# Three-layer graph convolution on one core: the third layer gathers rows stored as high and low f32r parts

## The reference

```python
def _gcn_layer(h_in, W, b, src, dst, norm_edge, n_nodes):
    h = h_in @ W
    msg = h[src] * norm_edge[:, None]
    agg = jax.ops.segment_sum(msg, dst, num_segments=n_nodes)
    return agg + b
...
deg = jax.ops.segment_sum(jnp.ones_like(dst, dtype=x.dtype), dst, num_segments=n)
dinv = jnp.where(deg > 0, jax.lax.rsqrt(deg), 0.0)
norm_edge = dinv[src] * dinv[dst]
h = x
for W, b in ((W1, b1), (W2, b2), (W3, b3)):
    h = jax.nn.relu(_gcn_layer(h, W, b, src, dst, norm_edge, n))
...
x = _layernorm(x + h, axis=-1)
```

## Time and profile before

| | us |
|---|---|
| median of three runs | 2473.04 |
| span of the profiled execution | 2904.7 |
| first layer's windows and before | up to 1165 |
| second layer | 1165 to 2346 |
| third layer | 2346 to 2904.7 |

### The profile page before, as it was taken

How to read it: one execution, slowest core, us unless ns; L and a number is a source line. 1 busy time by engine, 2 the same in 40 slices (tenths; PEclk the granted TensorE clock), 3 DMA queues, 4 the chain that set the end, 5 groups by cost and what they waited for, 6 DMA issues and landing times.

```text
span 2904.7 us, 33204 instructions
## 1 busy us (share of the span) xinstructions
PE 2414.3 (83%) x10765; PEld 1582.4 (54%) x10765; DVE 846.7 (29%) x1155; ACT 721.3 (25%) x1501; POOL 1757.6 (61%) x1768
## 2 busy tenths in 40 slices
PE   7866687788888789789788888979888789899897
PEld 6744465556565566344343444434444367777676
DVE  8875122112121211222222222222221223333333
ACT  6411222222122221122121222212221023333332
POOL 4366655556555564666667666666666756555553
PEclk9778899999899999899899898989999889999999
DMA  5445555555555555667666676767767645556663
GB/s 184 140 127 185 162 146 159 150 153 160 150 152 155 160 156 153 189 205 207 203 200 208 190 211 203 215 193 204 210 202 224 199 137 157 150 147 184 183 195 97
DMA packets 219959, 508.70 MB, mean 175 GB/s; under 512 B 38444, under 2 KB 106915, under 8 KB 219827
## 3 DMA queue, kind: packets, MB, share of 16 engines
q0 software_dynamic: 117216, 365.08, 44.1%
q1 hardware_dynamic: 83955, 109.08, 11.1%
q10 hardware_dynamic: 18656, 32.75, 3.7%
HBM read 433.60 MB, written 73.16 MB: 174 GB/s over the span
## 4 chain that ended last, share of the span: by engine, by line
PE 52%; another core or an unknown queue 22%; issue 10%; DVE 6%; ACT 4%; POOL 3%; DMA 1%; ACTq 1%; POOLq 1%; DVEq 0%; SPq 0%
PE ps_acc L1668 11%; PE ps_d L1668 9%; PE ps_o L1717 6%; PE ps_acc L1664 5%; PE ps_d L1767 4%; PE ps_h L1756 4%; PE ps_T L1756 3%; POOL rows L739 3%; PE ps_e L1738 3%; PE ps_l L1738 3%; ACT rows_r L1447 2%; PE ps_d L1620 2%; PE ps_h L1708 2%; DVE sel L956 1%
## 5 line engine op out<-in xcount | busy, mean ns | idle before, releaser
L739 POOL DMA_INDIRECT rows<-table,idx x1249 | 1240.8, 993 | 709.2 <-issue 382.6
L739 POOL DMA_INDIRECT rows<-table_parts,idx x483 | 476.5, 987 | 336.1 <-PE ps_acc L1664 152.7
L1668 PE MATMUL ps_acc<-rows,sel 128*128 128x512 f32 (+2 forms) x1496 | 615.9, 532 | 61.8 <-DVE acc L1042 27.7
L956 DVE SCALAR_TENSOR_TENSOR sel<-ps_e,firsts,dstT 128x1152 f32<-128x1152 f32 (+1 forms) x214 | 302.5, 1414 | 1223.6 <-remote 430.6
L1668 PE MATMUL ps_d<-rows,sel 128*128 128x512 f32 (+2 forms) x1190 | 541.4, 571 | 13.0 <-DMA rows<-table,idx 9.2
L1668 PEld LDWEIGHTS ps_acc<-rows,sel 128*128 128x128 f32 x1496 | 300.8, 208 | 226.5 <-issue 172.4
L1668 PEld LDWEIGHTS ps_d<-rows,sel 128*128 128x128 f32 x1190 | 235.8, 206 | 171.1 <-issue 134.0
L1664 PE MATMUL ps_acc<-rows,sel 128*128 128x256 bf16 (+1 forms) x1533 | 252.3, 281 | 81.9 <-DVE acc L1042 66.8
L1717 PE MATMUL ps_o<-low,hT 128*128 128x512 f32 (+1 forms) x784 | 295.9, 523 | 27.2 <-ACT hT L1365 14.4
L1767 PE MATMUL ps_d<-big 128*128 128x256 bf16 x1470 | 241.1, 280 | 28.8 <-issue 28.6
L1756 PE MATMUL ps_T<-pairs_r,rows_r 128*128 128x512 f32 x686 | 236.2, 460 | 33.2 <-ACT rows_r L1447 21.6
(11 more groups left out here) (192 smaller groups left out, 1663.3 us busy)
## 6 DMA issues: line engine op xcount, KB each, us to landing
rows<-table,idx POOLq DMA_INDIRECT x1249
table<-made SPq DMA_DIRECT2D x49, 256.0 KB
acc<-table SPq DMA_DIRECT2D x49, 256.0 KB
built<-big SPq DMA_DIRECT2D x30, 384.0 KB
low<-built ACTq DMA_DIRECT2D x30, 384.0 KB
built_bytes<-big SPq DMA_DIRECT2D x54, 192.0 KB
low<-built_bytes ACTq DMA_DIRECT2D x54, 192.0 KB
table_parts<-big SPq DMA_DIRECT2D x24, 384.0 KB
```

The lines of the kernel that those rows point to most:

```text
L739: pool.indirect_dma_start(out=to, out_offset=None, in_=its[0:nodes, :], in_offset=bass.IndirectOffsetOnAxis(ap=idx[:, of, k:k + 1], axis=0 ...
L956: v.scalar_tensor_tensor(to[:, k:k + FRONT, :], numbers.unsqueeze(1).broadcast_to([P, FRONT, P]), firsts[:, bass.ds(t, 1)], dstT[:, bass.d ...
L1668: return mm(to[:, 0:w], sel[:, k, :], rows_of[phase][:, k, 0:w] if first is None else first, start=start, stop=stop)
```

## The change

The second layer's product leaves PSUM in two steps: ScalarE writes `ps_o * dinv`, rounded to f32r, as the high part, and VectorE writes what is left (`keep_low`) as the low part, for one tile, two windows later. SP stores both as one row of 512 words in `table_pairs`. The third layer gathers rows of 2 KB from there instead of 1 KB, its selection is made in f32r, and a slot is one f32r matmul of 512 columns into a PSUM bank whose halves VectorE adds up (`take_pairs`). The own row is no longer loaded in the third layer; a matmul of `pairs_r` with the identity adds it after the second slot. The six wide steps and the copy for `late` go. As the rows now fill `rows`, the ring moves into `low`, and the room for loaded blocks shrinks from two blocks to one: each piece has its own buffer and is loaded one block ahead.

```diff
+        rows_pairs = rows_r[:, :].rearrange("p (k w) -> p k w", w=2 * C)
+        with nc.sbuf_tensor("sel_r", [P, SLOTS, P], F32R) as sel_r:
...
-        with nc.sbuf_tensor("pairs_r", [P, 2, T, C], F32R) as pairs_r:
+        with nc.sbuf_tensor("pairs_r", [P, T, 2, C], F32R) as pairs_r:
...
-        whole = xs
-        low_r, high_r = pairs_r[:, 0, :, :], pairs_r[:, 1, :, :]
+        pairs = pairs_r[:, :, :, :].bitcast(F32).rearrange("p t i c -> p t (i c)")
...
                     def store(t, s):
-                        sp.wait_ge(made_ready, s + 1)
-                        its = made[:, 0:WIDTH[phase + 1]]
                         if phase == 1 and per == 1:
-                            its = whole[:, bass.ds(t, 1), :].rearrange("p a c -> p (a c)")
-                        sp.dma_start(table[phase + 1][bass.ds(t * P, P), :], its).then_inc(stored, 16)
+                            sp.wait_ge(pairs_ready, t + 1)
+                            sp.dma_start(table_pairs[bass.ds(t * P, P), :],
+                                         pairs[:, bass.ds(t, 1), :].rearrange("p a w -> p (a w)")).then_inc(stored, 16)
+                        else:
+                            sp.wait_ge(made_ready, s + 1)
+                            sp.dma_start(table[phase + 1][bass.ds(t * P, P), :], made[:, 0:WIDTH[phase + 1]]).then_inc(stored, 16)
...
-            def gather(phase, k, of, nodes=T * P, in_parts=False):
+            def gather(phase, k, of, nodes=T * P, in_parts=False, in_pairs=False):
                 to, its = rows_of[phase][:, k, 0:WIDTH[phase]], table[phase]
                 if in_parts:
                     to, its = rows_parts[:, k, :], table_parts[phase]
+                if in_pairs:
+                    to, its = rows_pairs.bitcast(F32)[:, k, :], table_pairs
                 g = next(i for i, s in enumerate(GROUPS) if k in s)
                 pool.indirect_dma_start(
                     out=to, out_offset=None, in_=its[0:nodes, :],
                     in_offset=bass.IndirectOffsetOnAxis(ap=idx[:, of, k:k + 1], axis=0)).then_inc(landed[g], 16)
...
+            def take_pairs(t, n, ps):
+
+                v_.wait_ge(window_done, n + 1)
+                v.scalar_tensor_tensor(y1[:, :], ps[:, 0:C], dinv[:, t:t + 1], b3b[:, :], ALU.mult, ALU.add).then_inc(y_g_scaled, 1)
+                v_.wait_ge(y_g_scaled, t + 1)
+                v.scalar_tensor_tensor(y1[:, :], ps[:, C:2 * C], dinv[:, t:t + 1], y1[:, :], ALU.mult, ALU.add).then_inc(sum_taken, 1)
...
-            def take_apart(turn, t, n):
-
-                its = whole[:, bass.ds(t, n), :]
-                v.tensor_copy(high_r[:, bass.ds(t, n), :], its).then_inc(highs_ready, 1)
-                v_.wait_ge(highs_ready, turn + 1)
-                v.tensor_tensor(low_r[:, bass.ds(t, n), :], its, high_r[:, bass.ds(t, n), :], ALU.subtract).then_inc(pairs_ready, 1)
+            def keep_low(t):
+
+                v_.wait_ge(highs_ready, t + 1)
+                v.scalar_tensor_tensor(pairs_r[:, t, 1, :], ps_o[:, 0:C], dinv[:, t:t + 1], pairs_r[:, t, 0, :],
+                                       ALU.mult, ALU.subtract).then_inc(pairs_ready, 1)
...
-                    take_sum(phase, n - 1, n - 1, True, ps_sums[1 - odd] if phase > 0 else ps_acc)
+                    if phase == 2:
+                        take_pairs(t - 1, n - 1, ps_sums[1 - odd])
+                    else:
+                        take_sum(phase, n - 1, n - 1, True, ps_sums[1 - odd] if phase > 0 else ps_acc)
                     if not last:
                         indices(next_base, 1 - odd)
                     elif phase < 2:
                         v.tensor_copy(idx[:, 1 - odd, :], early_src[:, :]).then_inc(idx_ready, 1)
-                    prepare(n, t, base, 1, sel_parts if in_parts else sel)
+                    prepare(n, t, base, 1, to)
+                    if phase == 1 and t >= 2:
+                        keep_low(t - 2)
...
                 def to_next(phase):
                     n = nth_of_windows(phase + 1, 0)
                     base = base_of(1)
-                    prepare_early(n, 0)
+                    to = sel_r if phase == 1 else sel
+                    prepare_early(n, 0, to)
                     take_sum(phase, n - 1, n - 1, True, ps_sums[(n - 1) % 2] if phase > 0 else ps_acc)
                     indices(base, 1 - WINDOWS[phase + 1] % 2)
-                    prepare_early(n, 1)
+                    prepare_early(n, 1, to)
+                    if phase == 1:
+                        for t in range(T - 2, T):
+                            keep_low(t)
...
-                        if o == 2 and not first:
-                            n = PAIRS_OF[0][1]
-                            v_.wait_ge(stored, 16 * T + 16 * n * i)
-                            take_apart(i - 1, n * (i - 1), n)
...
                 def finish_gathered(g, b):
                     t = GROUP * g + b
                     n = nth_of_windows(2, t)
-                    finish(t, n + 2, n + 2, of_gather(g, b))
+                    normalize_rest(sum_taken, n + 2, res[:, :], res_in, t, of_gather(g, b), y3[:, :], y3_free, y_ready)
...
                 act.wait_ge(o_done, s + 1)
                 if phase == 1 and per == 1:
-                    to = whole[:, bass.ds(t, 1), :].rearrange("p a c -> p (a c)")
-                else:
-                    to = made[:, 0:w]
-                    act.wait_ge(made_free, s + 1)
+                    for of in range(2):
+                        if t == OVER_BYTES[of]:
+                            act.wait_ge(tile_stored[of], 16 * len(PIECES) * (DENSE // 2 + 1))
+                    act.sem_inc(act_step, 1)
+                    nc.scalar.activation(pairs_r[:, t, 0, :], ps_o[:, 0:w], ACT.Copy, scale=dinv[:, t:t + 1]).then_inc(highs_ready, 1)
+                    return
+                act.wait_ge(made_free, s + 1)
                 act.sem_inc(act_step, 1)
-                nc.scalar.activation(to, ps_o[:, 0:w], ACT.Copy, scale=dinv[:, bass.ds(t, 1)]).then_inc(made_ready, 1)
+                nc.scalar.activation(made[:, 0:w], ps_o[:, 0:w], ACT.Copy, scale=dinv[:, bass.ds(t, 1)]).then_inc(made_ready, 1)
...
-            def piece_in(j, into, piece):
+            def piece_in(j, piece):
 
                 lo_h, hi_h = PIECES[piece]
-                its = blocks[into][:, lo_h:hi_h, :].rearrange("p h d -> p (h d)")
-                return its.bitcast(U8)[:, 0:(hi_h - lo_h) * P] if in_bytes(j) else its
-
-            def load_blocks(j, into, piece):
+                n = (hi_h - lo_h) * P
+                return loaded[piece].bitcast(U8)[:, 0:n] if in_bytes(j) else loaded[piece][:, 0:n]
+
+            def load_blocks(j, piece):
                 lo_h, hi_h = PIECES[piece]
                 its = built_bytes if in_bytes(j) else built
-                act.dma_start(piece_in(j, into, piece), its[j * P:(j + 1) * P, lo_h * P:hi_h * P]).then_inc(blocks_in[into], 16)
-
-            def widen(g, x, more=True):
+                act.dma_start(piece_in(j, piece), its[j * P:(j + 1) * P, lo_h * P:hi_h * P]).then_inc(blocks_in[piece], 16)
+
+            def widen(g, x):
 
                 d, piece = divmod(x, len(PIECES))
                 lo_h, hi_h = PIECES[piece]
-                whole_x = DENSE_OF * len(PIECES) * g + x
-                act.wait_ge(blocks_in[d % 2], 16 * len(PIECES) * (DENSE_OF // 2 * g + d // 2 + 1))
-                if not (isinstance(g, int) and whole_x < 2):
+                j = DENSE_OF * g + d
+                whole_x = len(PIECES) * j + piece
+                act.wait_ge(blocks_in[piece], 16 * (j + 1))
+                if whole_x >= 2:
                     act.wait_ge(dense_piece, whole_x - 1)
                 act.sem_inc(act_step, 1)
                 nc.scalar.activation(ring[piece % 2][:, 0:hi_h - lo_h, :].rearrange("p h d -> p (h d)"),
-                                     piece_in(DENSE_OF * g + d, d % 2, piece), ACT.Copy).then_inc(widened, 1)
-                if more:
+                                     piece_in(j, piece), ACT.Copy).then_inc(widened, 1)
+                if j + 1 < DENSE:
                     act.wait_ge(widened, whole_x + 1)
-                    load_blocks(DENSE_OF * g + d + 2, d % 2, piece)
+                    load_blocks(j + 1, piece)
...
-                act.wait_ge(made_free, T + 1)
-                nc.scalar.activation(made[:, 0:C], ps_o[:, 0:C], ACT.Copy, scale=dinv[:, T - 1:T]).then_inc(late_ready, 1)
                 for of in range(2):
                     act.wait_ge(tile_stored[of], 16 * len(PIECES) * (DENSE // 2 + 1))
-                for piece in range(len(PIECES)):
-                    load_blocks(1, 1, piece)
                 widen(0, 0)
...
+                if in_pairs:
+                    return mm(to[:, 0:2 * C], sel_r[:, k, :], rows_pairs[:, k, :] if first is None else first, start=start, stop=stop)
...
+                    if own is not None and k == ORDER[1]:
```

(13 more changed lines are left out.)

118 lines of the change are left out of this document (65 added, 53 removed).

## The result

| | before | after |
|---|---|---|
| median | 2474.24 us (4 runs) | 2408.46 us (4 runs, 2405.69 to 2411.2) |
| ratio, 95% interval | | 0.9726 (0.9712 to 0.9739) |
| profiled span | 2904.7, profiled again 2471.5 | 2405.7 |

The change saves 65.8 us, 2.7%. The forecast was 2426 us, 47 us less, with a range of 2388 to 2466: the range holds the result, the gain is 19 us larger than forecast.

The account below looks back on a forecast made before the run. The prediction took TensorE to bound the third layer. Its terms, -70 slots, +4 GpSimd, +8 doubled rows, +7 ScalarE, +7 seam, -3 second layer, sum to -47 us: 2473 to 2426 us, range 2388 to 2466.

Parts of the forecast that it names:

- Slots, -70: Third layer, TensorE: 357 slots fall from 0.44 to 0.23 us, less 5 us for own-row matmuls; net -70 us.
- Rival E: Third-layer slots: an f32r matmul takes two passes, 0.46 us, after all; 2497 us, chance 0.05.
- GpSimd, +4: Third layer: gathers at 19.6 us a window are no longer covered by TensorE's 19.2; +4 us, between 0 and 8.
- Doubled rows, +8: Third-layer DMA queues: doubled row bytes make windows with bf16 blocks exceed TensorE's time; +8 us, between 0 and about 48.
- Rival C: Third layer: DMA engines become the bound and their packets do not overlap; 2450 us, chance 0.22.
- ScalarE's stops, +7: Third layer, between windows: TensorE waits longer for block widening behind a square root; +7 us, between 0 and 14.
- The seam, +7: Between layers two and three: tile 47's store waits for its low half, delaying the first gather; +7 us, -1.5 to 10.
- The second layer, -3: Second layer: without VectorE's wide splits, gathers beside them are no longer slowed; -3 us, between -15 and +3.
- mostly slack: Second layer: the delay of some 3 us at each of five wide-split places was taken as mostly slack.
- B: Full gain: gathers quicker than 1.25 us unprofiled, no DMA bound, seam partly hidden, splits' room wholly used; 2395 us, chance 0.12.
- A: The forecast itself, whole kernel: 2426 us, own range 2405 to 2448, chance 0.52.
- D: Third layer: block loads issued only one block ahead land late behind full gather queues; 2502 us, chance 0.09.

Follow-up runs that it names:

- experiment 2: Changed kernel with the third layer's slots as f32 matmuls of 256 columns over the high halves alone, except each window's first slot: 2464.35 us, ratio 0.9951.
- Experiment 3: Changed kernel with one gather less in each third-layer window but the first: 2399.57 us, ratio 0.9682.
- Experiment 4: Changed kernel gathering 1 KB rows instead of 2 KB in the third layer, as many gathers and still 512-column matmuls: 2407.5 us, ratio 0.9714.
- experiment 8: Changed kernel with ScalarE widening two pieces of each third-layer group before the square roots instead of behind them: 2405.52 us, ratio 0.9715.
- Experiment 5: Changed kernel with tile 47's low half made before the third layer's first selection instead of behind window 48's sum: 2400.66 us, ratio 0.9698.
- experiment 7: Changed kernel with five wide copy and tensor_tensor pairs put back on VectorE in the second layer: 2418.71 us, ratio 0.9776.
- experiment 6: Changed kernel without the own-row matmul in the third layer: 2405.79 us, ratio 0.9719.
- experiment 12: Changed kernel with tile 47's low part early and ScalarE widening first, plus dense-tile one-hots by eight short comparisons instead of two: 2373.56 us, ratio 0.9591.

## Why the prediction was right or wrong

**Slots, -70: right.** A slot is one record at 0.23 us; TensorE's busy time in the layer fell by 66 us between the two comparable profiles; experiment 2 gives 71 us back to TensorE. Rival E is out by the rows.

**GpSimd, +4: right mechanism, its window read too short.** "It is late next" held, and more than that: it never pauses again. The term had 329 gathers; there are 337, since eight of them started ahead of the stretch that was counted, so a window is 16.0 x 1.25 = 20.1 us and not 19.6. And the first rows were not there early: the slack counted for the first windows had gone at the seam. Experiment 3 prices GpSimd with the seam at some 9 us, where the forecast had 4 + 7.

**Doubled rows, +8: wrong.** Experiment 4 measures it at 1 us, within the error. The step that failed took five microseconds at 303 GB/s for a limit. (The 6.9 us a window of its first estimate are 6.7 by its own factors, 1.92 MB at 3.5 us; nothing hangs on it.) Late in the layer the page shows 344 and 347 GB/s in two slices of 60 us, and TensorE waits 1.3 us for rows in both together. Landing takes a gather 4.7 us (median) from its issue against 3.8 for all of the kernel before's, and that is hidden, as groups are asked for ahead. The Trainium skill (DMA: Bandwidth & Descriptors, Where 436 GB/s comes from) has about 358 GB/s as the limit of a core; the slices just named stay below it, and by that rule the term would have been nothing. Rival C is out.

**ScalarE's stops, +7: right as a term, worth less.** They grew by 6.7 us, as the forecast had it, but experiment 8 takes 7.6 us of them away, gets 7.3 us more of waits for rows, and leaves the layer's length as it was: a stop is covered by GpSimd, which fetches on through it.

**The seam, +7: right.** Experiment 5 gives 7.8 us back with the mechanism of the forecast, the store of tile 47 behind window 48's selection. It is right partly by luck: the clean profile shows that the old pause was 2.87 us and not the 13.3 of the earlier trace rows, and that the rows now start only 1.3 us ahead of the dense matmuls. A second part was not foreseen: TensorE waits for rows there and its granted clock is 0.62 over the first 13 us of the layer, where it was 0.87. By stretches it is 0.50 to 0.52, the lower level (1.2 GHz), from 1967 to 1977 us, after TensorE had been busy for 6.5 of the 12 us up to 1967; before the change the clock was back at 1.00, the upper level (2.4 GHz), 6 us into the layer. An estimate of the price is (0.87 - 0.62) x 13, some 3 us. With the rows 8.6 us sooner (experiment 5) the same 13 us show 0.87 again.

```profile
1979.00:1992.00 13.00, 12.95 (x51) 10.67 (x51) 1.54 (x2) 4.46 (x3) 9.70 (x11) 0.87 0.63 187
```

```profile
1964.00:1977.00 13.00, 9.13 (x21) 6.44 (x22) 0.00 (x0) 3.67 (x3) 9.95 (x11) 0.62 0.81 257
```

```profile
1964.00:1977.00 13.00, 12.98 (x50) 10.60 (x51) 1.42 (x1) 4.55 (x4) 9.94 (x11) 0.87 0.90 297
```

(first 13 us of the third layer, before profiled again, after, and in experiment 5; the columns are those of the stretches above.)

**The third layer's sum.** -70 for TensorE, +6.7 stops, +7.8 for rows, +3 for the clock give -53; measured -51.7. The forecast had -44 for the same; the DMA's 8 us are the difference. That the rest fits is partly luck: 4 + 7 for GpSimd and the seam stand against 7.8 + 3 of waits and clock.

**The second layer, -3: wrong, the largest miss.** 14.1 us were won ahead of the first dense matmul; 1.7 of them are the shorter way from the last product to it (5.9 to 4.1 us), which the forecast counted. Some 12 remain, and experiment 7 gives 10.3 of them back by nothing but the five wide pairs. The step that failed was "mostly slack". The delay itself was read nearly rightly, some 3 us at each of five places: the held time fell by 11.7 us in all, and layer two's gathers end 12.4 us sooner (table above). But GpSimd has no slack in layer two. The source of that is the choice at the start: stream rates were taken from the stalled profile rightly, busy shares were taken from it too, and 66% for GpSimd was the stalls. The same row would have told it: 784.34 us busy and 779 x 0.30 of issue are 1018 of 1181 us, and the 163 us left are less than the 432 of stalls that were known to lie somewhere. The low halves on VectorE, one of 0.48 us a window, read PSUM and hold no gather: no cost, as forecast. The two misses have the same sign, 8 us and 11 us (14.1 for 3), and are the 19 us by which the gain was larger.

**Rivals.** B (2395) and A (2426) lie on both sides of the result. B's first reason, gathers quicker than 1.25 us without a profile, has no room, since after's profiled span is the timed median within 3 us; its other one, no DMA bound, held. D: after, no widening waits for a block's load in the list of waits. D's "the trace shows no such wait" overlooks some entries: the list of the first profile puts 13.6 us of ScalarE's waits in the third layer down to such loads, that of the second 47.7. Whether these were the loads or the ring buffer, for which each widening also waits, the lists don't tell.

What stays open: experiment 6 gave 2.7 us where TensorE's share was expected to be covered, experiment 8 gave 2.9. Neither is clear of the two intervals, and the third layer's length in the profiles (440.1, 439.9 and 440.8 us) shows neither. Which engine sets the pace of layer one in experiment 12 was not followed.

## What to carry to other kernels

Before a busy share is read as slack, add an engine's busy and issue time over the stretch: if they fill it, it is the bound, whatever the share says (here 77% busy was 100% of the pace). Where a profile's span is well above the timed runs, take only paces from it and have it profiled again before slack is argued. Keep VectorE's operations short, or one operand in PSUM, wherever GpSimd issues gathers beside them.

## What the runs showed of the hardware

A gather's issue on GpSimd takes 0.95 us. If it starts during an operation of VectorE with two inputs in SBUF, it is held and ends 0.82 us behind the end of that operation: 672 of the 680 gathers that started during a bf16 comparison of 1.78 us, in all profiles together, and likewise beside a tensor_tensor or scalar_tensor_tensor in f32, where a gather took up to 3.66 us. The wide copies, with one input in SBUF, hold it too (nine gathers, 1.56 to 2.41 us). An operation with an input in PSUM doesn't: of 970 gathers that started in the first 0.46 us of the selection's 1.41, none took over 0.96. Nor do the statistics of the layer norm (0.4 us, one input in SBUF): 135 gathers, none over 0.96. Pieces of 0.3 to 0.5 us hold a gather by 0.1 to 0.2 us (median), 0.4 at most. The Trainium skill (SBUF — State Buffer, Who interferes with whom) says that an operation with two SBUF inputs contends with a GpSimd instruction that reads SBUF, and one with at most one SBUF input outside the two-port modes does not: both agree with the rows. Its inference that a tensor_tensor leaves descriptor generation alone does not hold for these indirect gathers, which the forecast had noted from the earlier trace rows.
